# A one-hot gather that multiplies all bf16 parts at once, and another order of the steps on every engine

## What is computed

```python
scores = jnp.einsum('bnf,fo->bn', inputs, score_proj)
_, top_idx = jax.lax.top_k(scores, k)                 # k = 375 of 750 tokens
sel_feat = jnp.take_along_axis(inputs, top_idx[:, :, None], axis=1)
h = sel_feat * jax.nn.sigmoid(sel_scores)[:, :, None]
# then h + attention(layernorm(h)): 4 heads of 16, softmax over
# (q + u_bias) @ k.T + rel_shift((q + v_bias) @ p.T), and a projection
```

## Time and profile before

| | |
|---|---|
| median of 3 runs | 3182.33 us (3175.29 to 3184.69) |
| the profiled execution's own time | 3183.66 us |
| its span (first to last instruction) | 3181.9 us |
| PE, matmuls | 2969.3 us busy, 93% |
| PEld, weight loads | 2136.3 us, 67% |
| DVE | 2585.7 us, 81% |
| ACT | 1806.3 us, 57% |
| POOL | 1307.3 us, 41% |
| mean granted TensorE clock | 0.953 |

### The profile page before, as it was taken

How to read it: one execution, slowest core, us unless ns; L and a number is a source line. 1 busy time by engine, 2 the same in 40 slices (tenths; PEclk the granted TensorE clock), 3 DMA queues, 4 the chain that set the end, 5 groups by cost and what they waited for, 6 DMA issues and landing times.

```text
span 3181.9 us, 72607 instructions
## 1 busy us (share of the span) xinstructions
PE 2969.3 (93%) x24964; PEld 2136.3 (67%) x24964; DVE 2585.7 (81%) x7699; ACT 1806.3 (57%) x4484; POOL 1307.3 (41%) x1368
## 2 busy tenths in 40 slices
PE   0699999999999979999799999999999999999995
PEld 0488888888888844444577777666666666666663
DVE  4788888888888658887778886688888888888873
ACT  0255555555555535555567775466666666666662
POOL 1435353545454324443100001356555555555542
PEclk9999999999999979999778988899999999999996
DMA  4100000000000000000000001432332233233210
GB/s 149 37 22 17 23 16 23 16 23 16 23 16 16 2 1 1 1 1 1 1 1 2 1 1 19 54 42 41 50 50 42 44 50 46 42 50 50 42 23 4
DMA packets 69714, 84.24 MB, mean 26 GB/s; under 512 B 19592, under 2 KB 64968, under 8 KB 68968
## 3 DMA queue, kind: packets, MB, share of 16 engines
q1 hardware_dynamic: 68328, 79.20, 13.8%
q10 hardware_dynamic: 1024, 0.39, 0.1%
HBM read 29.93 MB, written 3.17 MB: 10 GB/s over the span
## 4 chain that ended last, share of the span: by engine, by line
PE 34%; DVE 13%; POOL 2%; issue 2%; ACT 1%; DMA 0%; SPq 0%; POOLq 0%; DVEq 0%; ACTq 0%
PE psum L2310 4%; PE psum L2296 3%; PE psum L2324 3%; PE psum L2283 3%; PE psum L1641 3%; PE psum L2347 3%; DVE qe_top L2763 3%; PE psum L1670 2%; PE psum L1658 2%; POOL qe_root L3013 2%; DVE qe_y L2741 1%; PE psum L1712 1%; PE psum L1703 1%; PE psum L2259 1%; DVE qe_fo L2741 1%
## 5 line engine op out<-in xcount | busy, mean ns | idle before, releaser
L2763 DVE TENSOR_REDUCE qe_top<-psum 125x1 f32<-125x375 f32 (+2 forms) x896 | 499.4, 596 | 102.5 <-PE psum L2283 101.2
L2570 ACT ACTIVATE qe_E<-psum 125x375 f32<-125x375 f32 (+1 forms) x896 | 454.7, 531 | 210.7 <-PE psum L2283 203.7
L2283 PE MATMUL psum<-bconst 125*125 125x125 bf16 (+2 forms) x1792 | 466.5, 260 | 0.0
L606 PE MATMUL psum<-Q,K 96*125 96x125 f32 (+3 forms) x2304 | 404.4, 311 | 0.5 <-ACT E L817 0.4
L606 PEld LDWEIGHTS psum<-Q,K 96*125 96x125 f32 (+1 forms) x2304 | 334.5, 189 | 24.5 <-issue 1.2
L1156 POOL TENSOR_TENSOR Q<-rot 64x375 f32<-64x375 f32 (+1 forms) x256 | 305.7, 1213 | 71.5 <-DVE rot L957 59.4
L2310 PE MATMUL psum<-qe_Q,qe_K 97*125 97x375 bf16 (+2 forms) x1536 | 316.6, 284 | 5.2 <-DMA qe_Q<-qe_maxT 2.4
L817 ACT ACTIVATE E<-psum 125x500 f32<-125x500 f32 x384 | 226.2, 589 | 165.2 <-PE psum L626 163.9
L2296 PE MATMUL psum<-qe_K,qe_Q 96*125 96x375 bf16 (+2 forms) x1536 | 308.6, 282 | 3.3 <-DVE qe_top L2763 3.1
L812 ACT CAST half_scores<-psum 125x250 bf16<-125x250 f32 x384 | 140.6, 366 | 221.9 <-PE psum L611 194.8
L2283 PEld LDWEIGHTS psum<-bconst 125*125 125x125 bf16 x1792 | 248.6, 139 | 11.4 <-issue 7.7
(11 more groups left out here) (341 smaller groups left out, 7255.1 us busy)
## 6 DMA issues: line engine op xcount, KB each, us to landing
qe_Q<-qe_parts SPq DMA_DIRECT2D x192, 187.5 KB, 4.6
s_row<-scores SPq DMA_DIRECT2D x32, 366.2 KB
qe_K<-qe_parts SPq DMA_DIRECT2D x192, 46.9 KB, 4.5
x_tokens<-x SPq DMA_DIRECT2D x32, 187.5 KB
x_chunks<-x SPq DMA_DIRECT2D x4, 750.0 KB
E<-x SPq DMA_DIRECT2D x4, 750.0 KB
out<-qe_hout SPq DMA_DIRECT2D x32, 93.8 KB
weights<-weights_in SPq DMA_DIRECT2D x1, 2363.5 KB, 24.4
```

Source lines behind the costliest of these rows:

```text
L606: nc.tensor.matmul(out[:, first * TP:(first + n) * TP].rearrange("p (o q) -> p o q", o=n), t.K[0:rows(h), par, h, jt * TP:(jt + 1) * TP], ...
L2283: return nc.tensor.matmul(out, B("ident_b")[0:TP, 0:TP], rhs, start=False, stop=True, skip_group_check=True)
L2570: nc.scalar.activation(E[:, e % 2, a:a + width], bank[0:TP, 4 + n % 2, 0:width], ACT.Exp).then_inc(e_done, 1)
L2763: nc.vector.tensor_reduce(dst, src, AX, ALU.max).then_inc(m_read, 1)
```

## The change

The gather multiplies each one-hot tile with all three parts side by side: 192 columns in one matmul for output tiles 0 and 1. The third tile would pass the end of the bank (384 + 192 columns of 512), so there two parts go together (128 columns) and the third part is a matmul of its own, which adds to the first part's columns. ScalarE no longer copies the sum; it copies the second part's columns to a new tile `second`. VectorE adds first and second part, and then the third part for tiles 0 and 1. `count` waits in addition for `one_hot` of the batch before.

```diff
             def gather(b, par, it):
...
+                together = 3 if it < NT - 1 else 2
                 for c in range(CI):
-                    for i in range(3):
-                        last = nc.tensor.matmul(bank[0:TP, 0, it * D:(it + 1) * D],
-                                                t.hot[:, c, it * TP:(it + 1) * TP], t.x3[:, c, i, :],
-                                                start=c == 0 and i == 0, stop=c == CI - 1 and i == 2)
+                    hot, at = t.hot[:, c, it * TP:(it + 1) * TP], it * 3 * D
+                    last = nc.tensor.matmul(bank[0:TP, 0, at:at + together * D], hot,
+                                            t.x3[:, c, 0:together, :].rearrange("p i f -> p (i f)"),
+                                            start=c == 0, stop=c == CI - 1, skip_group_check=True)
+                    if together == 2:
+                        last = nc.tensor.matmul(bank[0:TP, 0, at:at + D], hot, t.x3[:, c, 2, :],
+                                                start=False, stop=c == CI - 1, skip_group_check=True)
...
-            def keep_rows(b, par):
+            def keep_second(b, par):
                 act.wait_ge(gathered, b + 1)
-                wait(act, xn_ready, b)
-                nc.scalar.copy(t.h_new[:], bank[0:TP, 0, 0:NT * D]).then_inc(h_copied, 1)
+                wait(act, h_copied, b)
+                nc.scalar.copy(t.second[:]..., <second part's columns of bank 0>).then_inc(second_kept, 1)
...
+            def keep_rows(b, par):
...
+                dve.wait_ge(second_kept, b + 1)
+                wait(dve, xn_ready, b)
+                own.link(dve, nc.vector.tensor_tensor(rows, parts[:, :, 0, :], t.second[:].rearrange("p (t f) -> p t f", t=NT), ALU.add))
+                nc.vector.tensor_tensor(rows[:, 0:NT - 1], rows[:, 0:NT - 1], parts[:, 0:NT - 1, 2, :],
+                                        ALU.add).then_inc(h_copied, 1)
```

On VectorE the counts 0 to 5 of batch r are spread over the round, `keep_rows` stands between `negate(b3, 8)` and `maximum(b3, 9)`, `statistics` two pieces later. On GpSimd a round is now rotations 2, root, rotations 3, both `other_parts`, rotations 0 and 1, and two waits between these pieces are set to fit:

```diff
                 if h == 3:
-                    wait(pool, x_split, capped(b + 2, nb))
-                    wait(pool, rstd_ready, b + 1)
+                    wait(pool, rstd_ready, capped(b + 2, nb))
...
-                wait(pool, Q_rows, (b - 1) * 4 + 4)
+                wait(pool, Q_rows, (b - 1) * 4 + 2)
```

More of the change, by code:

```diff
@@ L913, in count @@
                     own.wait(dve)
+                    wait(dve, hot_ready, b)
                     dve.wait_ge(row_loaded, (b + 1) * 16)
@@ L1065, in step @@
[L1065 to L1066 removed]
+                    divide(bs[4], s[4])
                 if on[3]:
[L1068 to L1070 removed]
+                    most(bs[3], s[3], 6)
+                if on[0]:
+                    take_scores(bs[0], s[0])
                 if on[3]:
[L1072 to L1076 removed]
@@ L1132, in step @@
                 if on[3]:
-                    maximum(bs[3], s[3], 0)
-                    add_next(bs[3], s[3])
-                    negate(bs[3], s[3], 0)
-                if on[0]:
-                    take_scores(bs[0], s[0])
-            rounds(dve, step, 5, own, nb)
+                    maximum(bs[3], s[3], 6)
+                    negate(bs[3], s[3], 6)
+                if on[2]:
+                    rotate(bs[2], s[2], 1, 1)
+                if on[3]:
+                    most(bs[3], s[3], 7)
@@ new lines, in step @@
+                if on[4]:
+                    add_out(bs[4], s[4])
+                if on[0]:
+                    count(bs[0], s[0], 0)
+                if on[3]:
+                    maximum(bs[3], s[3], 7)
+                    negate(bs[3], s[3], 7)
+                if on[0]:
+                    gate_tokens(bs[0], s[0])
+                if on[3]:
+                    most(bs[3], s[3], 8)
+                if on[0]:
+                    count(bs[0], s[0], 1)
+                if on[3]:
+                    maximum(bs[3], s[3], 8)
+                    most(bs[3], s[3], 9)
+                    negate(bs[3], s[3], 8)
@@ new lines, in step @@
+                if on[1]:
+                    keep_rows(bs[1], s[1])
+                if on[3]:
+                    maximum(bs[3], s[3], 9)
+                    negate(bs[3], s[3], 9)
+                if on[1]:
+                    statistics(bs[1], s[1])
+                if on[3]:
+                    most(bs[3], s[3], 10)
+                if on[0]:
+                    count(bs[0], s[0], 2)
+                if on[3]:
+                    maximum(bs[3], s[3], 10)
+                    most(bs[3], s[3], 11)
+                    negate(bs[3], s[3], 10)
@@ new lines, in step @@
+                if on[2]:
+                    multiply_next(bs[2], s[2])
+                if on[1]:
+                    normalise(bs[1], s[1])
+                if on[3]:
+                    maximum(bs[3], s[3], 11)
+                    negate(bs[3], s[3], 11)
+                if on[2]:
+                    most(bs[2], s[2], 0)
+                    keep_next(bs[2], s[2])
+                    add_next(bs[2], s[2])
+                if on[0]:
+                    count(bs[0], s[0], 3)
+                if on[2]:
+                    maximum(bs[2], s[2], 0)
+                    negate(bs[2], s[2], 0)
+                    most(bs[2], s[2], 1)
@@ new lines, in step @@
+                if on[0]:
+                    count(bs[0], s[0], 4)
+                if on[3]:
+                    lower_next(bs[3], s[3])
+                if on[2]:
+                    maximum(bs[2], s[2], 1)
+                    negate(bs[2], s[2], 1)
+                    most(bs[2], s[2], 2)
+                if on[0]:
+                    count(bs[0], s[0], 5)
+                if on[1]:
+                    rotate(bs[1], s[1], 0, 0)
+                if on[2]:
+                    maximum(bs[2], s[2], 2)
+                    most(bs[2], s[2], 3)
+                    negate(bs[2], s[2], 2)
@@ L1141, in _ @@
+                if on[1]:
+                    rotate(bs[1], s[1], 0, 1)
+                if on[2]:
+                    maximum(bs[2], s[2], 3)
+                    negate(bs[2], s[2], 3)
+                    most(bs[2], s[2], 4)
+                if on[0]:
+                    one_hot(bs[0], s[0], 0)
+                if on[3]:
+                    weigh_values_next(bs[3], s[3])
+            rounds(dve, step, 4, own, nb)
         @block.gpsimd
```

392 lines of the change are left out of this document (163 added, 229 removed).

## The result

The changed kernel takes 3198.63 us (median of 8 runs, 3191.55 to 3210.71), the kernel before 3182.44 (8 runs on the same chip, 3175.29 to 3185.01): a ratio of 1.0049 (95% interval 1.0032 to 1.0067). It is 0.5% slower where 1.5% faster was forecast. The profiled execution took 3198.7 us, its span is 3196.9, the mean granted clock 0.954.

A forecast was written before the change was run, and what follows sets the result against it. TensorE was taken to bound the loop at 31.65 us a round. 31 distances of 1.39 us (43.1) and 6 us at start and end make 49 off 3183.66: 3135 us, range 3118 to 3165.

The forecast's parts named there:

- The gather: TensorE's one-hot matmuls: wider ones cut the gather from 3.08 to 1.69 us, saving 1.39 us a round.
- The third rival: Wide matmuls don't hide the next tile's load: gather 2.65 us, gain 0.43 a round, time 3164 us; chance 0.05.
- the price that the prediction worked out from the Trainium skill: Gather by the page's 81 to 87 ns a pair: saving 2.3 us a round, time 3107 us; chance 0.01.
- hand-offs: TensorE's loop: the old order loses 0.6 us a round between pieces, and the new order keeps that loss.
- ScalarE and the adds: ScalarE swaps one copy for an equal one, within 0.1 us; VectorE's two PSUM adds cost 0.65 us, bounds 0.5 to 0.8.
- GpSimd and the counts: GpSimd's moved work overlapping VectorE's counts: about half are hit as before, so zero, bounds -1.2 to +1.9 us a round.
- The order: Walk through TensorE's new list, 29.6 us end to end: no long wait, tightest place `scores(b2,2)` with 0.3 us spare.
- Start and end: Before and after the loop: first result 9 us earlier, end saves 2.4 us less; together -6 us, unsure by 6.
- The second one, on the other side: VectorE's idle time doesn't shrink, 28.45 + 3.85 = 32.3 us a round, time 3198 us; chance 0.07.
- The first one: VectorE partly holds the loop, its waits staying at 2.5 us: round 31.0 us, time 3157 us; chance 0.20.
- The count's mean over 1.35: Sign on VectorE: mean count expected at 1.20 us; above 1.35, the new place of GpSimd's work is to blame.
- VectorE under 1 us idle: Sign in the loop: the prediction is wrong if VectorE has less than 1 us idle left a round.

The follow-up runs named there:

- e12: Changed kernel with all four GpSimd rotations cut to one column, so it computes something else; 3127.50 us, 0.9820 of the kernel before.
- e1: Changed kernel with VectorE's first three `one_hot` moved to right behind count 5, where GpSimd is idle; 3172.43 us, 0.9953 of the kernel before.
- e3: Changed kernel with the first three `one_hot` moved behind count 5 and GpSimd's rotations 3 waiting for `normalise`; 3170.07 us, 0.9938 of the kernel before.
- e4: Kernel before with only the wide gather, the second-part copy and the two adds, in the old order; 3160.64 us, 0.9923 of the kernel before.
- e13: Wide gather in the old order (e4) with all four GpSimd rotations cut to one column, computing something else; 3133.70 us, 0.9851 of the kernel before.
- e11: Changed kernel with GpSimd's rotations 0 waiting for the first three `one_hot` and rotations 3 for `normalise`; 3157.04 us, 0.9906 of the kernel before.
- e9: Wide gather in the old order (e4) with `most` of unit 8 moved ahead of count 3 on VectorE; 3192.49 us, 1.0027 of the kernel before.
- e8c: Kernel before with six idle GpSimd additions of 64x375 near the start of the round; 3178.60 us, 0.9989 of the kernel before.

## Why the prediction was wrong

**The gather: right.** 1.64 us where 1.69 was worked out, 0.49 and 0.66 where 0.50 and 0.68. The third rival (load not hidden, 0.8 us a tile) falls. So does the price that the prediction worked out from the Trainium skill (TensorE: Matmul & The Clock Gate, Back-to-back issue gap), about 2.1 us for the new gather, where the trace has 1.64. e12's round is 1.66 us shorter than the old one: 1.44 are the gather's (3.08 less 1.64), and the other 0.2 are left for hand-offs, of whose 0.6 us the prediction had kept all.

**ScalarE and the adds: right.** The copy of the second parts takes 0.34 us (0.32 before), the adds 0.63 together (0.65), and GpSimd doesn't lengthen them.

**"GpSimd and the counts": the step that failed.** It was put at zero. It had one term, the counts, and that one was even better than zero: six counts take 6.30 us and not 7.23. The step had no term for `one_hot` and `normalise`, nor for any other VectorE instruction than the counts. Yet the new lists lay there: rotations 0 and 1 start as VectorE comes to `one_hot` 0, rotations 3 as it comes to `normalise`. In the old lists GpSimd's long pieces never meet the two, which is why their rows in the trace of before, 411 and 307 ns, carry no sign of a price; the GpSimd instructions that do run over a `one_hot` there are those of the root, three columns each. The longest:

```profile
542.38 1.05 DVE L925 TENSOR_SCALAR one_hot<-fconst,rank 125x375 bf16<-125x375 f32 x3
...
542.91 0.91 POOL L1180 TENSOR_TENSOR rstd<-rstd,minus_half 125x3 f32<-125x3 f32 x1
```

It is nearly as long as a rotation and costs nothing, so length alone doesn't do it. An overlap that the trace doesn't show needs bounds from the nearest row, and this one was given none. The nearest was the count: 0.5 us longer under GpSimd. Nine instructions at 0.5 would have been +4.5 us at worst, six of them +3.0; measured are +2.1 for `one_hot` and +1.5 for `normalise`. That bound would have held by luck: five of the nine are caught, and each of the five gets some 0.7 us longer, not 0.5. With the adds (+0.63), the gate (+0.13) and the counts (-0.9) the printed lengths grow by 3.4 us a round. Printed lengths overlap by some 0.1 us, so the time in which VectorE works grows by less, from 27.84 to 30.67, where 28.45 had been forecast.

How much of the missing 2.06 us a round (32.32 less 30.26) belongs to which group is known in part. Clearing `one_hot` gives back 0.96 us (e1), clearing both 0.94 (e3), since the moved GpSimd work catches others. Only without the long rotations is all of it back, 2.35 us (e12).

In the Trainium skill, GPSIMD Engine Reference (Specifications) names two kinds of VectorE instructions that contend, those with two SBUF inputs and those in a 2-port perf mode; SBUF — State Buffer (SBUF: two separate sides) says that the shared ports are locked for a whole instruction and that the loser stands still. `one_hot` and `normalise` read one SBUF tensor (beside scalars for each partition) and are slowed all the same, so by the Trainium skill they would be of the second kind, which the prediction left out; no run here shows the mode itself. The traces agree in kind: waits on either side, one for each instruction. They don't agree that the lock spans the whole instruction: `one_hot` and rotations alternate at 0.99 and 1.06 us from one `one_hot` to the next (563.241, 564.231, 565.295), while alone they take 0.32 and 0.94 start to start, 1.26 together.

**The order: wrong by that.** The walk took VectorE's pieces at their old lengths and named 0.3 us before `scores(b2,2)` as the tightest place. TensorE waits elsewhere, 1.25 us at `turn_most` and 0.43 at `turn_tokens`, the second straight behind a lengthened group, the first 2 us behind one (`one_hot` ends at 566.42, `most` starts at 568.38) with VectorE at work in between. With the lengths put right (e12) the walk holds: no waits, 29.97 us for 30.26.

**Start and end.** The gather begins at 100.63 (99.9 forecast), `xT` is kept at 111.28 (109.6), but the first result is there at 184.75 and not at 174.5. One reading of the prediction was wrong here without harm. It took the low clock of the first gather from the 0.84 of 103 to 137 us; that mean comes from 126 to 137 us, where the granted clock is 0.50, and the profile prints 1.00 for 103.2 to 109.3. What speaks for the low level is the price: the same matmuls take 107 ns start to start at 104 us and again at 127 us, under a granted 0.50, but 57 to 59 at 125. The new gather takes the 3.4 us there that were forecast. The start, too, has the long groups; all engines' timeline:

```profile
100.63 2.29 PE L527 MATMUL psum<-x_three,one_hot 125*125 125x192 bf16 x13 [22.19 <-DVE one_hot L935]
...
108.38 1.91 DVE L967 TENSOR_SCALAR xn<-h_new,mean_var,rstd 125x64 f32<-125x64 f32 x3 [1.37 <-POOL rstd L1205]
...
111.28 0.66 ACT L783 ACTIVATE xT<-psum,weights 64x375 f32<-64x375 f32 x1 [6.49 <-PE psum L540]
...
117.07 2.49 DVE L935 TENSOR_SCALAR one_hot<-fconst,rank 125x375 bf16<-125x375 f32 x3
```

e12 has the first result at 175.86, so 8.9 of the 10.2 us go with GpSimd's rotations as well. The end saves 24.9 us against full rounds (3 x 32.33 - 72.1) and not 17; in e12 it is 31 x 29.97 - 910.7 = 18.4. The sum: 31 x (32.33 - 30.26) = 64.2, less 7.9 at the end, plus 10.2 at the start, is 66.5 us, and the last result came at 1162.15 instead of about 1096.

**The rivals.** The second one, on the other side, named 32.3 us and 3198; measured are 32.32 and 3198.6, and VectorE's work and waits are past its limit of 31.85. But it got there on another way: it had the work at 28.45 and the waits unchanged at 3.85, where the work is 30.67 and the waits are 1.65. It said "1.5 with all six counts hit" and so came near, with the wrong instructions. Its chance of 0.07 was too small because GpSimd's price had been set to zero in all cases. The first one, 31.0 us and 3157, is what e4 does (31.05, 3160.6). That too is mostly GpSimd: with short rotations the same order takes 30.20 (e13), and the counts then fall from 7.20 to 6.31 us.

**The signs.** "The count's mean over 1.35: the new place of GpSimd's work is to blame" pointed the wrong way; the mean fell and GpSimd was to blame. "VectorE under 1 us idle" wasn't met either, with 1.65. What told it was the length of every group of VectorE beside that of before. The later stages moved by 2.1 us, within the 3 allowed.

## What to carry to other kernels

Where pieces of VectorE and GpSimd are moved against each other, list the pairs that will overlap, and give each VectorE instruction whose tensors all lie in SBUF one GpSimd instruction's length as the upper bound of its price, however small it is; a duration from the old trace holds only for the old neighbours. Put work that reads PSUM, or a merged instruction, over GpSimd's long stretches, and keep groups of short SBUF instructions away from them. Where GpSimd's work is moved away from one of them, look up what it falls on next: in e3 that took back what `normalise` gave. After a change of order, compare the mean length of every group before asking who waits for whom.

## What the runs showed of the hardware

- A VectorE instruction of 0.41 us (`one_hot`) or 0.31 us (`normalise`) takes mostly 1.03 to 1.19 us when GpSimd runs instructions of 0.97 us beside it, and ends 0.2 us (`one_hot`) or 0.05 us (`normalise`) after one of them. Even 0.16 us (`s_loc`, six columns) became 0.62 (e11), and 0.17 us (`s_next`, twelve columns) 0.87 (e3).
- The wait is for each instruction and not for each element: three `one_hot` of 375 columns took 3.18 us, one of 1125 columns, by another operation, 1.32, with and without GpSimd, which then waited itself (0.97 to 2.17 us). A count of 0.98 us became 1.35 in the kernel after and up to 1.69 in e9.
- GpSimd's instruction of three columns (125x3) does no harm though it lasts 0.91 us. VectorE instructions with an operand in PSUM aren't held either: in e8c a `maximum` runs from 521.930 to 522.335 and a `rotate` with one operand in SBUF from 526.920 to 527.452, both inside a GpSimd add (521.866 to 522.840, 526.670 to 527.654), at their usual 0.41 and 0.53 us. Nor are all that read SBUF alone: the reciprocal of `den`, twelve columns, takes its 0.23 us at 523.093 in e8c, inside an add from 522.918 to 523.895. `negate`, one column, keeps its 0.22 us inside a rotation of the kernel after (562.675 to 562.891 in 562.187 to 563.159), and so does a reduction over the 192 columns of `qk_next` in e3, 0.34 us (538.791 to 539.133 in 538.679 to 539.674). What sets these apart from `s_loc` and `s_next` stays open.
- A matmul of 192 bf16 columns with a weight load of its own takes 82 ns start to start, one of 128 and one of 64 together 110 ns (0.66 us for six pairs): at 128 columns and fewer the price stands at about 55 ns and no longer follows the columns. That fits the load that every matmul has here; no run leaves the load out.
